# Last stage of a graph network kernel: inverse counts loaded per block, attributes in pieces of nine groups, node layers in another order, 27 packed tiles a run

## Chip, cores and metric

The kernel runs on one core of a Trainium2 chip. Its time is the device time of one execution in microseconds (us), lower is better; the median of three executions is quoted. The engines of the core are TensorE (PE; its weight loads are PEld), VectorE (DVE), ScalarE (ACT), GpSimd (POOL) and SyncE (SP), which issues most of the DMAs.

## Reference

Two layers of message passing over a graph with 6250 nodes of 128 features and 106250 edges sorted by target. The change lies in the second layer, cut here to what it computes:

```python
C = 0.5 * (jnp.cos(edge_weight * (jnp.pi / 5.0)) + 1.0)
C = C * (edge_weight < 5.0)
h = jax.nn.silu(edge_attr @ mlp_w1 + mlp_b1)         # (edges, 64) @ (64, 128)
W = (h @ mlp_w2 + mlp_b2) * C[:, None]
xf = layernorm_relu(x) @ lin1_w
agg_sum = jax.ops.segment_sum(xf[src] * W, dst, num_segments=n_nodes)
cnt = jax.ops.segment_sum(jnp.ones((msg.shape[0],)), dst, num_segments=n_nodes)
agg = agg_sum / jnp.maximum(cnt, 1.0)[:, None]
out = jax.nn.silu(agg @ lin2_w + lin2_b) @ lin_w + lin_b
x = x + out
```

Edges with a weight of 5 or more add nothing. The inputs draw weights from 0 to 20.12, so about a quarter of the edges count ("active" ones).

## Kernel before

The nodes are cut into 49 blocks of 128. Three passes follow one another. Passes 1 and 2 (the first layer, and the rows of the second) go over the edges in slots; beside the slots the kernel counts neighbours into matrix tiles in SBUF (`adjacency`), multiplies them with split tables (L2023), and packs the active edges: the edges lie in 8 runs of 26 groups of 512, and each run's active edges are moved together into `CAP` = 28 tiles of 128, with their attributes turned (64 partitions) in the DRAM tensor `packed_attr`. A test on the chip takes a slow general path where a run has more than 128 times `CAP` active edges; the largest run of these inputs has 3347, as counted from the reference's weights.

The **last stage** (pass 3, code from L2133 on for PE) is a loop over `PG` = 56 packed groups h of four tiles. Its steps for a group:

- POOL issues four indirect gathers of 128 table rows each into one of four ring slots (L975). It waits until `summed` says that the group four before is summed.
- SP loads the group's attributes, 64 partitions by 512 (L773), two groups ahead, into one of three buffers `attr_T`.
- PE multiplies them by `mlp_w1` (`hidden`, L2133, one group ahead), ACT applies silu (L1207), PE makes the filter from a bias product (L2069) and four products (L2073).
- DVE builds a one-hot tile (L1521) and multiplies filter, cut and gathered rows (`packed_message`, four instructions of L1735).
- PE runs six products whose result nothing reads (`unused_products`, L2151, into the bank that the next sum overwrites) and sums the message by target (`sum_packed`, L2140); DVE adds the four windows to the accumulator `acc` (`packed_flush`, L1749).

As soon as the edges of a node block j are all in (`PACKED_UPDATES`, worked out from the shapes) its **node layer** is run beside the groups: DVE scales the identity by the block's inverse counts (L1636), PE spreads them with a product by ones (`scales`, L2056), ACT copies that to SBUF (L1198), DVE multiplies the columns of `acc` by it into `z_T` (L1643), PE multiplies by `lin2` (u, L2062), ACT applies silu (L1201), PE multiplies by `lin` (v, L2065), and DVE adds the bias (L1647) and the block's x (L1651); SP stores the row block (L710) and loads the x of the next (L722). 47 of the 56 groups carry a node layer; two blocks come after the loop. Engines follow their program in order, and semaphores tie them. The order around a group's node layer on DVE is:

```python
packed_onehot(h)
packed_message(h)
if h - 1 in PACKED_UPDATES:
    node_3(PACKED_UPDATES[h - 1], 1)      # bias and x
if h in PACKED_UPDATES:
    diagonal(PACKED_UPDATES[h])
if h:
    packed_flush(h - 1)
if h in PACKED_UPDATES:
    node_3(PACKED_UPDATES[h], 0)          # z_T
```

The filter of group g waits for the message of group g - 2, `v` of block j for the finished row of block j - 1, and the load of x for block j for the row of block j - 3.

## Time and profile before

| | us |
|---|---|
| median of 3 executions | 1630.23 (1620.26 to 1630.88) |
| the profiled execution, device time | 1629.68 |
| its span, first to last instruction | 1627.9 |
| mean granted TensorE clock | 0.905 |
| last stage, first gather to the end | 1271.8 to 1627.9 |

The profiled execution lies 0.6 us below the median. Its span is 1.8 us shorter than its device time, which is what lies around the instructions. Times in rows count from the first instruction. A granted clock of 1 is 2.4 GHz, one of 0.5 is 1.2 GHz, and what lies between is a share of time at either.

### The profile page before, as it was taken

The numbers are of one execution on the slowest core, as the hardware profiler recorded it, in microseconds if no ns is written. First come the engines' busy times: TensorE is split into PE (matmuls) and PEld (weight loads), VectorE is DVE, ScalarE is ACT, GpSimd is POOL, SyncE is SP. The second block draws the span as 40 slices with busy tenths as digits, with TensorE's granted clock in tenths as the row PEclk, the third lists the DMA queues.
The fourth block names the chain that finished last, engine by engine and source line by source line (L and its number), as shares of the span: only waits on it lengthen the run. The fifth ranks groups of instructions, "written<-read, shape, count | busy, mean of one in ns | idle before, by whom it ended". The sixth has DMA issues, their size and how long they took to land.

```text
span 1627.9 us, 35768 instructions
## 1 busy us (share of the span) xinstructions
PE 1374.4 (84%) x11813; PEld 1199.7 (74%) x11813; DVE 813.2 (50%) x2806; ACT 724.9 (45%) x2025; POOL 1123.8 (69%) x1158
## 2 busy tenths in 40 slices
PE   3457999988988899884799999998997899999996
PEld 2246888878888788874799888988986566666664
DVE  3984444545455555443444445434534355555553
ACT  2856665656655666652454345335421221222221
POOL 7577777777777777757667776777675575666661
PEclk9955999999999999985899999999998798998897
DMA  4323455544545655536567657766753232333331
GB/s 115 84 60 87 136 154 172 158 149 141 144 128 157 175 159 155 154 85 184 131 190 207 190 151 199 208 163 173 195 143 83 73 90 77 88 91 84 87 87 34
DMA packets 245643, 217.40 MB, mean 134 GB/s; under 512 B 150236, under 2 KB 201568, under 8 KB 244941
## 3 DMA queue, kind: packets, MB, share of 16 engines
q1 hardware_dynamic: 210125, 142.61, 31.0%
q0 software_dynamic: 35328, 72.42, 16.4%
q8 instruction: 99, 1.62, 0.4%
q14 instruction: 91, 0.75, 0.1%
HBM read 156.61 MB, written 58.31 MB: 132 GB/s over the span
## 4 chain that ended last, share of the span: by engine, by line
PE 57%; DVE 16%; issue 9%; POOL 7%; DMA 4%; ACT 3%; DVEq 1%; SPq 1%; ACTq 1%; POOLq 0%
PE ps_product L2023 21%; PE ps_banks L1971 9%; POOL ring L975 7%; PE ps_banks L1983 5%; PE ps_pack L2000 5%; PE ps_banks L2073 5%; DVE acc L1749 3%; DMA table_in<-node_table 2%; PE ps_banks L2140 2%; PE ps_banks L1988 2%; PE ps_banks L2151 2%; PE ps_node L2062 2%; DVE ring L1735 2%; ACT adjacency L1132 1%; ACT packed_T L1178 1%
## 5 line engine op out<-in xcount | busy, mean ns | idle before, releaser
L975 POOL DMA_INDIRECT ring<-node_table,src_idx x880 | 858.2, 975 | 324.1 <-issue 255.5
L2023 PE MATMUL ps_product<-adjacency,table_parts 128*128 128x232 bf16 x4116 | 508.6, 269 | 0.0
L2023 PEld LDWEIGHTS ps_product<-adjacency,table_parts 128*128 128x128 bf16 x4116 | 403.3, 103 | 12.7 <-DVE table_parts L1557 0.2
L1132 ACT CAST adjacency<-ps_banks 128x550 f32 x448 | 298.5, 666 | 213.9 <-PE ps_banks L1988 190.3
L1971 PE MATMUL ps_banks<-onehot,ring 128*128 128x64 f32 x1760 | 251.9, 291 | 73.0 <-issue 46.6
L975 POOL DMA_INDIRECT ring<-node_table,packed_src x224 | 212.4, 948 | 129.5 <-issue 58.7
L1971 PEld LDWEIGHTS ps_banks<-onehot,ring 128*128 128x128 f32 x1760 | 235.4, 208 | 90.0 <-issue 77.5
L1178 ACT COPY packed_T<-ps_pack 67x64 f32 x832 | 173.4, 208 | 160.5 <-PE ps_pack L2000 54.9
L1546 DVE TENSOR_SCALAR code_onehot<-code_iota,code_T 128x600 bf16<-128x600 bf16 x448 | 169.0, 389 | 130.9 <-PE ps_banks L1988 130.1
L1983 PE MATMUL ps_banks<-code_onehot,lo_onehot 128*128 128x300 bf16 x896 | 200.7, 309 | 20.7 <-ACT adjacency L1132 20.5
L2000 PE MATMUL ps_pack<-pack_onehot,edge_in 128*67 128x64 f32 x1664 | 148.7, 236 | 14.9 <-ACT packed_T L1178 14.5
L2000 PEld LDWEIGHTS ps_pack<-pack_onehot,edge_in 128*67 128x67 f32 x1664 | 130.9, 151 | 17.3 <-issue 16.7
L1735 DVE SCALAR_TENSOR_TENSOR ring<-ps_banks,packed_dst,ring 128x128 f32<-128x128 f32 x224 | 63.2, 345 | 120.3 <-PE ps_banks L2073 114.8
L1983 PEld LDWEIGHTS ps_banks<-code_onehot,lo_onehot 128*128 128x128 bf16 x896 | 97.6, 122 | 27.0 <-DVE code_onehot L1546 14.9
L1988 PEld LDWEIGHTS ps_banks<-code_onehot,lo_onehot 128*128 128x128 bf16 x864 | 101.2, 117 | 21.5
L1988 PE MATMUL ps_banks<-code_onehot,lo_onehot 128*128 128x25 bf16 x864 | 112.6, 221 | 0.0
L1537 DVE TENSOR_TENSOR acc<-acc,ps_banks 128x64 f32 x220 | 47.9, 218 | 100.4 <-PE ps_banks L1971 86.7
L1198 ACT COPY scale_all<-ps_banks 128x128 f32<-128x128 f32 x49 | 13.0, 265 | 189.0 <-PE ps_banks L2056 189.0
L1521 DVE TENSOR_TENSOR pack_onehot<-iota_b,rank 128x256 f32<-128x256 bf16 x208 | 86.0, 418 | 16.4 <-PE ps_pack L2000 16.4
L1521 DVE TENSOR_TENSOR onehot<-iota_b,rel 128x256 f32<-128x256 bf16 x220 | 90.8, 413 | 2.7 <-issue 2.7
L2073 PE MATMUL ps_banks<-mlp_w_sb,hidden_T 128*128 128x128 f32 x448 | 81.6, 338 | 0.0
L2073 PEld LDWEIGHTS ps_banks<-mlp_w_sb,hidden_T 128*128 128x128 f32 x448 | 68.8, 234 | 14.2 <-ACT hidden_T L1207 8.1
(277 smaller groups left out, 1499.0 us busy)
## 6 DMA issues: line engine op xcount, KB each, us to landing
kept_tiles<-adjacency SPq DMA_DIRECT2D x84, 406.0 KB
adjacency<-kept_tiles SPq DMA_DIRECT2D x84, 406.0 KB
edge_in<-in_edge_attr_dram SPq DMA_DIRECT2D x207, 128.0 KB
ring<-node_table,src_idx POOLq DMA_INDIRECT x880
packed_attr<-packed_T SPq DMA_DIRECT2D x8, 896.0 KB
attr_T<-packed_attr SPq DMA_DIRECT2D x56, 128.0 KB, 3.0
node_table<-row_out SPq DMA_DIRECT2D x98, 64.0 KB
ring<-node_table,packed_src POOLq DMA_INDIRECT x224
```

The lines of the kernel that those rows point to most:

```text
L975: gps.indirect_dma_start(to, None, table[c], bass.IndirectOffsetOnAxis(index, 0)).then_inc(gathered[s], 16)
L1132: nc.scalar.copy(adjacency[:, b, :, bass.ds(at, n)].rearrange("p (t b) n -> p t b n", t=2), chunk_banks(m).rearrange("p t (b n) -> p t b n ...
L1178: nc.scalar.copy(packed_T[:, run % 2, bass.ds(at[k], WINDOW)], ps_pack[0:RF, k * WINDOW:(k + 1) * WINDOW]).then_inc(packed_out, 1)
L1521: return vec.tensor_tensor(to, iota[:], of.unsqueeze(2).to_broadcast([P, CHUNKS, WINDOW]), ALU.is_equal)
L1546: vec.tensor_scalar(code_onehot[:, m % CODE_SETS, :], code_iota[:], code_T[:].bitcast(F32)[:, at:at + 1], None, ALU.is_equal).then_inc(chu ...
L1735: last = vec.scalar_tensor_tensor(out=ring[:, s, k, :], in0=ps_filter[:, h % 2, k * P:(k + 1) * P], scalar=packed_cut[:, CHUNKS * h + k:CH ...
L1971: last = mm(ps_window, ring[:, s, k, :], onehot[:, n % 2, k, :], start=(k == 0), stop=(k == CHUNKS - 1))
L1983: last = mm(chunk_banks(m)[:, half, :], left(m), code_onehot[:, m % CODE_SETS, half * HIGH * SPAN:(half + 1) * HIGH * SPAN], start=True, s ...
L1988: last = mm(chunk_banks(m)[:, half, :].rearrange("p (b n) -> p b n", n=SPAN)[:, :, 0], left(m - 1), shared.rearrange("p (b n) -> p b n", n ...
L2000: last = mm(ps_pack[0:RF, k * WINDOW:(k + 1) * WINDOW], edge_in[:, s, k, :], pack_onehot[:, q % 2, k, :], start=True, stop=True)
L2023: product = mm(ps_product[:, 0:COLS], table_parts[:, k, part, :], adjacency[:, buffer_of(c, tile), k, :], start=(k == 0 and part == 0), st ...
L2073: last = mm(ps_filter[:, slot, k * P:(k + 1) * P], hidden_T[:, slot, k, :], mlp_w2_sb[:], start=False, stop=(k == CHUNKS - 1))
```

## The change

- `CAP` goes from 28 to 27, so the last stage has 54 groups and 216 gathers for 56 and 224. 47 of the 54 carry a node layer.
- The inverse counts are turned and stored once, at the end of the start phase, into a DRAM tensor `inv_rows`. In the last stage `load_x(3, j)` loads the block's row of it, spread to 128 partitions, together with its x. `diagonal`, `scales` and the copy on ACT are gone.
- The attributes come in six pieces of nine groups (64 partitions by 4608) into two halves that lie over `adjacency`. The first two are loaded near the end of pass 2, once the last product with `adjacency` is done; the others in the loop, at h = 11, 20, 29 and 38.
- On PE u comes behind the filter and v behind the sum. On DVE `z_T` comes straight behind the flush and the bias and x behind `z_T`.
- After the loop the two left blocks no longer go one after the other; the second has banks of its own for u and v.
- The unused products are kept, six a group, but read `table_parts` in place of `adjacency`, with 256 columns for 232.

```diff
-SUPERS, CAP = 8, 28
+SUPERS, CAP = 8, 27
+PIECE = 9
...
+        attr_pieces = adjacency[0:R].rearrange("r s b n -> r (s b n)").bitcast(F32)[:, 0:2 * PIECE * GROUP].rearrange(
+            "r (s e) -> r s e", s=2)
...
+        def u_bank(j):
+
+            return (ps_pack if j in PACKED_TAIL[1:] else ps_node)[:, 0:P]
+
+        def v_bank(j):
+            return ps_count[:, 0 if j in PACKED_TAIL[1:] else 2, 0:F]
...
                     sp.dma_start(x_in[:, b, :], x_mid[j * P:(j + 1) * P, :]).then_inc(x_block[b], 16)
+                    sp.dma_start(scale_in[:, b, :], inv_rows[j, :].partition_broadcast(P)).then_inc(x_block[b], 16)
...
-            def load_attr_T(h):
-                s = h % 3
-                wait(sp, hidden_done, h - 2)
-                sp.dma_start(attr_T[:, s, :], packed_attr[:, h * GROUP:(h + 1) * GROUP]).then_inc(attr_T_loaded[s], 16)
+            def load_piece(i):
+                if i < PG // PIECE:
+                    wait(sp, hidden_done, PIECE * (i - 1))
+                    sp.dma_start(attr_pieces[:, i % 2, :],
+                                 packed_attr[:, i * PIECE * GROUP:(i + 1) * PIECE * GROUP]
+                                 ).then_inc(piece_loaded[i % 2], 16)
...
-                            for h in range(2):
-                                load_attr_T(h)
+                        if c == 2 and n == SLOT_COUNT[2] - REST_SLOTS + 2:
+                            sp.wait_ge(block_used[2], NB * TILES)
+                            for i in range(2):
+                                load_piece(i)
...
                 for h in range(PG):
-                    if h + 2 < PG:
-                        load_attr_T(h + 2)
+                    if h % PIECE == 2 and h > PIECE:
+                        load_piece(h // PIECE + 1)
...
-            def diagonal(j):
-                wait(dve, scale_done, j)
-                vec.tensor_scalar(scale_diag[:], ident[:], inv_count[:, j:j + 1], None, ALU.mult).then_inc(diag_ready, 1)
...
                 if part == 0:
-                    dve.wait_ge(scale_ready, j + 1)
+                    dve.wait_ge(x_block[b], 16 * in_set(b) + 32 * (j // SETS + 1))
                     wait_acc()
-                    vec.tensor_tensor(z_T[:, b, :], columns(j), scale_all[:], ALU.mult).then_inc(z_ready[3], 1)
+                    vec.tensor_tensor(z_T[:, b, :], columns(j), scale_in[:, b, :], ALU.mult).then_inc(z_ready[3], 1)
...
                     packed_message(h)
-                    if h - 1 in PACKED_UPDATES:
-                        node_3(PACKED_UPDATES[h - 1], 1)
-                    if h in PACKED_UPDATES:
-                        diagonal(PACKED_UPDATES[h])
                     if h:
                         packed_flush(h - 1)
                     if h in PACKED_UPDATES:
                         node_3(PACKED_UPDATES[h], 0)
+                    if h - 1 in PACKED_UPDATES:
+                        node_3(PACKED_UPDATES[h - 1], 1)
...
+            pe.wait_ge(inv_ready, 1)
+            turn(ps_pack[0:NB, 0:P], inv_count[:], ident[:]).then_inc(inv_turned, 1)
...
-                        mm(ps_agg[:, bank, 0:COLS], table_parts[:, 0, 0, :], adjacency[:, 0, 0, :],
+                        mm(ps_agg[:, bank, 0:2 * F], table_parts[:, 0, 0, :], table_parts[:, 0, 1:3, :].rearrange("p t f -> p (t f)"),
                            start=True, stop=True)
...
-                    if h - 1 in PACKED_UPDATES:
-                        node_3(PACKED_UPDATES[h - 1], 0)
                     if h == 0:
                         unused_products(1, WARM_UP)
                         pe.wait_ge(row_ready[2], NB)
                     edge_filter(h, h % 2)
                     if h - 1 in PACKED_UPDATES:
-                        node_3(PACKED_UPDATES[h - 1], 1)
+                        node_3(PACKED_UPDATES[h - 1], 0)
                     if h:
                         wait(pe, flushed[3], CHUNKS * (h - 2))
                         unused_products((h - 1) % 2, KEEP_WARM)
                         sum_packed(h - 1)
-                    if h in PACKED_UPDATES:
-                        scales(PACKED_UPDATES[h])
+                    if h - 1 in PACKED_UPDATES:
+                        node_3(PACKED_UPDATES[h - 1], 1)
```

PE in the loop before, one group with a node layer and the start of the next (lin_sb stands for `lin2` with z_T and for `lin` with z_row):

```order
L2133 MATMUL ps_pack<-attr_T,mlp_w_sb 128x512
L2062 MATMUL ps_node<-z_T,lin_sb 128x128
L2069 MATMUL ps_banks<-b_parts,b_ones 128x512
L2073 MATMUL ps_banks<-mlp_w_sb,hidden_T 128x128 x4
L2065 MATMUL ps_banks<-lin_sb,z_row 128x128
L2151 MATMUL ps_banks<-adjacency,table_parts 128x232 x6
L2140 MATMUL ps_banks<-onehot,ring 128x64 x4
L2056 MATMUL ps_banks<-scale_diag,ones 128x128
L2133 MATMUL ps_product<-attr_T,mlp_w_sb 128x512
```

The same stretch of PE in the changed kernel:

```order
L2149 MATMUL ps_pack<-adjacency,mlp_w_sb 128x512
L2083 MATMUL ps_banks<-b_parts,b_ones 128x512
L2087 MATMUL ps_banks<-mlp_w_sb,hidden_T 128x128 x4
L2075 MATMUL ps_node<-z_T,lin_sb 128x128
L2168 MATMUL ps_banks<-table_parts 128x256 x6
L2157 MATMUL ps_banks<-onehot,ring 128x64 x4
L2079 MATMUL ps_banks<-lin_sb,z_row 128x128
L2149 MATMUL ps_product<-adjacency,mlp_w_sb 128x512
```

The product with z_T moved from ahead of the filter to behind it, the one with z_row behind the sum, and the spreading product is gone.

DVE in the loop before, from one z_T to the first window of the next flush:

```order
L1643 TENSOR_TENSOR z_T<-acc,scale_all 128x128
L1521 TENSOR_TENSOR onehot<-iota_b,packed_dst 128x256
L1735 SCALAR_TENSOR_TENSOR ring<-ps_banks,packed_dst,ring 128x128 x4
L1647 TENSOR_TENSOR row_out<-ps_banks,lin_b_all 128x128
L1651 TENSOR_TENSOR row_out<-row_out,x_in 128x128
L1636 TENSOR_SCALAR scale_diag<-ident,inv_count 128x128
L1742 TENSOR_LOAD packed_base_i
L1749 ISA
L1749 TENSOR_TENSOR acc<-acc,ps_banks 128x64
```

The same stretch of DVE in the changed kernel:

```order
L1663 TENSOR_TENSOR z_T<-acc,scale_in 128x128
L1667 TENSOR_TENSOR row_out<-ps_banks,lin_b_all 128x128
L1669 TENSOR_TENSOR row_out<-row_out,x_in 128x128
L1545 TENSOR_TENSOR onehot<-iota_b,packed_dst 128x256
L1753 SCALAR_TENSOR_TENSOR ring<-ps_banks,packed_dst,ring 128x128 x4
L1760 TENSOR_LOAD packed_base_i
L1767 ISA
L1767 TENSOR_TENSOR acc<-acc,ps_banks 128x64
```

The bias and x left the stretch between message and flush, and the scaled identity is gone.

## Rows read from the trace of the kernel before

**Rows 1.** The page, chain that ended last, shares of the whole span.

```profile
PE 57%; DVE 16%; issue 9%; POOL 7%; DMA 4%; ACT 3%; DVEq 1%; SPq 1%; ACTq 1%; POOLq 0%
```

**Rows 2.** Timeline of one group (start, length, engine, line, idle before it).

```profile
1453.88 0.49 PE L2062 MATMUL ps_node<-z_T,lin_sb 128*128 128x128 f32 x2 [0.29 <-DVE z_T L1643]
...
1455.62 0.39 PE L2065 MATMUL ps_banks<-lin_sb,z_row 128*128 128x128 f32 x2
1455.89 1.13 DVE L1735 SCALAR_TENSOR_TENSOR ring<-ps_banks,packed_dst,ring 128x128 f32<-128x128 f32 x4 [1.72 <-PE ps_banks L2073]
1456.93 0.28 DVE L1647 TENSOR_TENSOR row_out<-ps_banks,lin_b_all 128x128 f32<-128x128 f32 x1
...
1457.46 0.28 DVE L1636 TENSOR_SCALAR scale_diag<-ident,inv_count 128x128 f32<-128x128 f32 x1
...
1457.79 0.49 PE L2056 MATMUL ps_banks<-scale_diag,ones 128*128 128x128 f32 x2 [0.34 <-DVE scale_diag L1636]
1457.82 1.28 DVE L1749 TENSOR_TENSOR acc<-acc,ps_banks 128x64 f32 x4
...
1459.20 0.29 DVE L1643 TENSOR_TENSOR z_T<-acc,scale_all 128x128 f32<-128x128 f32 x1
...
1459.55 0.49 PE L2062 MATMUL ps_node<-z_T,lin_sb 128*128 128x128 f32 x2 [0.22 <-DVE z_T L1643]
```

**Rows 3.** Chain of waits of the last stage (start, length, engine, line).

```profile
1340.17 0.49 PE ps_node L2062 x2
...
1347.27 0.49 PE ps_node L2062 x2
...
1448.12 1.05 PE ps_product L2133 x2
1449.49 1.09 PE ps_banks L2073 x8
1450.58 0.60 PE ps_banks L2151 x6
1451.17 0.86 PE ps_banks L2140 x8
```

**Rows 4.** Stretches: busy us of PE, PEld, DVE, ACT, POOL; granted clock, DMA share, GB/s.

```profile
1300.00:1350.00 50.00, 46.52 (x254) 34.27 (x254) 25.71 (x101) 10.16 (x23) 35.02 (x38) 0.88 0.33 87
```

**Rows 5.** Timeline of the end of pass 2 and the stage's first groups.

```profile
1251.09 0.94 POOL L975 DMA_INDIRECT ring<-node_table,src_idx  x1 [0.30 <-issue]
...
1258.58 1.81 PE L1971 MATMUL ps_banks<-onehot,ring 128*128 128x64 f32 x8
...
1271.76 0.94 POOL L975 DMA_INDIRECT ring<-node_table,packed_src  x1 [19.74 <-DMA node_table<-row_out]
...
1276.79 0.39 PE L2069 MATMUL ps_banks<-b_parts,b_ones 3*128 3x512 bf16 x1
...
1280.49 0.95 POOL L975 DMA_INDIRECT ring<-node_table,packed_src  x1 [0.30 <-issue]
...
1283.04 1.13 DVE L1735 SCALAR_TENSOR_TENSOR ring<-ps_banks,packed_dst,ring 128x128 f32<-128x128 f32 x4 [3.08 <-DMA ring<-node_table,packed_src]
...
1299.30 1.01 POOL L975 DMA_INDIRECT ring<-node_table,packed_src  x1 [0.30 <-issue]
```

**Rows 6.** SP's queue around a store of 64 rows of 14,336 bytes.

```profile
1206.26 0.45 SPq L745 DMA_DIRECT2D packed_attr<-packed_T  x1
...
1207.38 2.09 SPq L710 DMA_DIRECT2D node_table<-row_out  x1
```

**Rows 7.** The stretch in which that store moved, columns as in Rows 4.

```profile
1207.40:1212.40 5.00, 5.00 (x56) 4.63 (x54) 0.67 (x6) 0.00 (x0) 3.58 (x4) 0.93 0.92 184
```

**Rows 8.** DMAs of the attributes, issue to landing, us min/median/max.

```profile
DMA to landing us min/median/max: 2.6/3.0/3.8
```

**Rows 9.** Timeline of the end.

```profile
1611.86 1.81 PE L2140 MATMUL ps_banks<-onehot,ring 128*128 128x64 f32 x8
...
1623.65 0.29 DVE L1651 TENSOR_TENSOR row_out<-row_out,x_in 128x128 f32<-128x128 f32 x1
```

More of the change, by code:

```diff
@@ L533, in gnn_kernel @@
         held = sem("held")
-        attr_T_loaded = [sem(f"attr_T_loaded_{s}") for s in range(3)]
+        piece_loaded = [sem(f"piece_loaded_{b}") for b in range(2)]
         edge_turned = sem("edge_turned")
@@ L696, in _, with store_inverse @@
             store_table(0)
+            def store_inverse(time):
+                sp.wait_ge(early_done, time + 1)
+                if time:
+                    sp.wait_ge(inv_stored, 16)
+                sp.dma_start(inv_rows, inv_out).then_inc(inv_stored, 16)
             def late_params():
@@ L841, in fast_path @@
                 first = NB - len(PACKED_TAIL)
-                store_row(3, first - 1)
-                for j in PACKED_TAIL:
-                    if j + 1 < NB:
-                        load_x(3, j + 1)
+                for j in PACKED_TAIL[1:]:
+                    load_x(3, j)
+                for j in range(first - 1, NB):
                     store_row(3, j)
@@ L1287, in general_path @@
                 start_sums(1)
+                act.wait_ge(inv_stored, 16)
+                act.wait_ge(inv_turned, 2)
+                nc.scalar.copy(inv_out, ps_pack[0:NB, 0:P]).then_inc(W12_ready, 1)
                 act.wait_ge(early_done, 2)
@@ L2051, in node_2 @@
                     mm(bank[:, 2 * P:2 * P + F], h2_T[:, b, :], lin1_sb[:], start=True, stop=True).then_inc(xf_done, 1)
-            def scales(j):
-                pe.wait_ge(diag_ready, j + 1)
-                wait(pe, row_ready[3], j)
-                mm(ps_count[:, 2, P:2 * P], ones[:], scale_diag[:], start=True, stop=True).then_inc(scale_done, 1)
             def node_3(j, part):
@@ L2061, in node_3 @@
                     pe.wait_ge(z_ready[3], j + 1)
-                    mm(ps_node[:, 0:P], lin2_sb[:], z_T[:, b, :], start=True, stop=True).then_inc(u_done, 1)
+                    wait(pe, u_ready, j)
+                    mm(u_bank(j), lin2_sb[:], z_T[:, b, :], start=True, stop=True).then_inc(u_done, 1)
                 if part == 1:
                     pe.wait_ge(u_ready, j + 1)
-                    mm(ps_count[:, 2, 0:F], z_row[:, b, :], lin_sb[:], start=True, stop=True).then_inc(v_done, 1)
+                    wait(pe, row_ready[3], j - 1 if j in PACKED_TAIL[1:] else j)
+                    mm(v_bank(j), z_row[:, b, :], lin_sb[:], start=True, stop=True).then_inc(v_done, 1)
             def edge_filter(g, slot):
@@ L2130, in hidden @@
                 def hidden(h):
-                    pe.wait_ge(attr_T_loaded[h % 3], 16 * (h // 3 + 1))
+                    piece, at = divmod(h, PIECE)
+                    if at == 0:
+                        pe.wait_ge(piece_loaded[piece % 2], 16 * (piece // 2 + 1))
                     wait(pe, hidden_ready, h - 1)
-                    mm(hidden_bank(h), mlp_w1_sb[:], attr_T[:, h % 3, :], start=True, stop=True).then_inc(hidden_done, 1)
+                    mm(hidden_bank(h), mlp_w1_sb[:], attr_pieces[:, piece % 2, at * GROUP:(at + 1) * GROUP],
+                       start=True, stop=True).then_inc(hidden_done, 1)
                 def sum_packed(h):
```

77 lines of the change are left out of this document (37 added, 40 removed).

## Prediction

> **What bounds the kernel now.** I read the chain that ended last first: 57% of it is PE, 16% DVE, 7% POOL [rows 1]. That is a mean over three passes, and the change touches almost only the last stage, 1271.8 to 1627.9. So I took the timeline of one of its groups and followed who waits for whom [rows 2]. PE starts u (L2062) at 1453.88 and again at 1459.55: a group with a node layer takes 5.67 us. What closes the circle is one chain over two engines: u, filter, message on DVE (1455.89), bias and x, scaled identity (1457.46), flush (1457.82, 1.28 us), z_T (1459.20), and again u, which waits for it. Neither engine alone is full. PE's own work in a group is, by the steps of the chain of waits [rows 3], 1.05 for `hidden`, 0.32 for the bias product (from 1449.17 to 1449.49), 1.09 for the filter, 0.60 for the unused products and 0.86 for the sum, 3.92 us; u adds 0.49, v 0.39 and the spreading product 0.49 [rows 2]. That is 5.29 of 5.67 us.
>
> Second, TensorE's clock. From 1300 to 1350 it was granted at 0.88 [rows 4], so about a quarter of that time ran at 1.2 GHz. A group in which it falls takes 7.10 us (1340.17 to 1347.27, [rows 3]) for 5.67: a fall costs 1.43 us. The loop runs from 1276.79 [rows 5] to the last sum at 1611.86 [rows 9], 335.1 us. 47 groups with a node layer at 5.67 (266.5) and 9 without at 3.92 (35.3) leave 33.3 us, some 23 falls.
>
> Third, POOL. The 1st and the 23rd gather of the stage start at 1271.76 and 1299.30 [rows 5]: while POOL waits for nothing, a gather takes 27.54 / 22 = 1.252 us and a group 5.01 us. Before, POOL had 0.66 us of slack in a group; it is the next bound behind the chain.
>
> **The change, part by part.**
>
> *Reordering.* z_T is still made behind the flush, but u now stands behind the filter, so the filter and with it the next message no longer wait for z_T. What is left of the old circle lacks u (0.43 from start to start), the scaled identity and the two row additions (1456.93 to 1457.82, 0.89): 5.67 - 0.43 - 0.89 = 4.35 us, under what PE itself needs. PE then needs 3.92 + 0.49 + 0.39 = 4.80, and the unused products with 256 columns for 232 add 10% of 0.60, 0.06: 4.86 us with a node layer, 3.98 without. DVE's work (message 1.13, flush 1.28, z_T 0.29, row additions 0.57, one-hot some 0.4) is under 4 us and its waits fit in: the flush waits for the sum, z_T and rows follow, and the next filter ends about 3 us after that sum. New on PE's way: v waits for the previous block's row, which DVE ends 2 to 3 us after the sum before, so about 2 us early; u waits for z_T with about 1 us to spare. Nothing queued behind them waits as long as these hold.
>
> *Sum for PE.* 47 x 4.86 + 7 x 3.98 = 256.3 us, from 1276.79: the last sum would end at 1533.1 at full clock and with no wait.
>
> *Sum for POOL.* 216 gathers. The last starts at 1271.76 + 215 x 1.252 = 1540.9. A message starts 2.55 us after its group's last gather (1280.49 to 1283.04, [rows 5]), so at 1543.5. Then message 1.13, flush 1.28, z_T 0.29, u 0.49 and the last sum 0.86: 1547.6. So POOL, not PE, is the nearer bound: 5.01 against 4.86 us in a group. PE has 14.5 us to lose in the whole loop before it counts.
>
> *Clock.* What will the falls be? Between none and the 0.41 a group of before (22 of them, 31.5 us). Before, PE stood still in every group for z_T; now it is busy 4.86 of 5.01 us, and only the 7 groups without a node layer leave 1 us. I take 10 falls, 14.3 us: those 7 places and a few after the holds below. The Trainium skill ("TensorE: Matmul & The Clock Gate", section "HAM oscillation") says that a kernel whose matmul bursts are parted by idle gaps falls back to the half clock, and a dense stream keeps the full one; the direction is that of my 10 against 22.
>
> *Attribute pieces.* As many bytes, but 64 rows of 18,432 bytes at a time. The nearest row is a store of 64 rows of 14,336: after it SP needed 2.09 us to issue its next DMA [rows 6], and for 5.0 us the DMA engines were 92% busy at 184 GB/s [rows 7]. A piece is 1.29 times as large: 6.4 us in which a gather may land late. The lower end is nothing, as the 128 KB loads (3.0 us from issue to landing, [rows 8]) and the gathers now share without a wait. I take the store's row, the only one with such long packets. The first hold then stops PE for up to 6.4 us. The three later ones meet a PE that already runs behind its gathers (it makes up 0.15 us in a group and 1 us in one without a node layer, some 2 us between two pieces), so I count one hold, 6.4 us. SP stands too, 2 to 4 us, and the loads of x and inverse behind the piece come later: they are issued almost two groups, 9.4 us, before z_T needs them, and take 1.0 us to issue and 3.0 to land, so 5.4 us are free.
>
> *Together.* 1533.1 + 14.3 + 6.4 = 1553.8 for the end of the last sum, later than POOL's 1547.6, so this one counts.
>
> *End.* Before, from the end of the last addition (1623.94, [rows 9]) to the span's end there were 4.0 us, the store. After the last sum come now flush and two z_T, of which the last waits for x of block 48: its load waits for row 45, about 0.8 us before the sum's end (1546.8 for 1547.6), and lands 4.0 us later; then z_T 0.3, u and v 0.8 each at the low clock, silu 0.4, additions 0.6, waits 0.4 and the store 4.0. That ends 10.4 us after the sum, for 14.2 before.
>
> *Pieces 0 and 1 in pass 2.* They go out at about 1241, together 12.8 us of transfer. PE summed the pass's last slot at 1258.58, its last gather was issued at 1251.09 [rows 5]; less 2.55 that is 5 us of cover. Between no delay and 7.9 us I take 1.5, since most held gathers land well ahead of that sum. *Start phase.* One transpose, one copy of 49 rows and a small store: a few tenths of a us beside work that the chain has anyway; nothing. One transpose less in each `turn_packed`, beside 27: nothing. The second load per block is 0.5 us on SP, which the attribute load of before took as well.
>
> Sum: 1553.8 + 10.4 + 1.5 = 1565.7 of span, and 1.8 around it: **1567 us** for the profiled 1629.68, which stands for the median (1630.23).
>
> **The rivals.**
>
> *Clock as before.* Nothing shows what density keeps the clock; the falls could stay at 0.41 a group. Then 31.5 for 14.3 us: 1585.
>
> *Every piece is paid in full.* If PE never runs behind, or a hold lasts longer than the row says, the loop pays 4 x 6.4 for 6.4 (+19.2) and pass 2 its 7.9 for 1.5: 1593. For it speaks the 92% of [rows 7]. A rule of the Trainium skill says more: "DMA: Bandwidth & Descriptors", section "Queues, rings and completion order", lets an engine change queues only between packets of several descriptors, so that a gather waits for the whole share of the piece that lies ahead of it. By that rule the hold is the transfer's 6.4 us each time, and the time 1593 unless the lag hides it; by the 128 KB loads alone it would be 1561. With the clock as before as well it would be 1610.
>
> *The load of x and inverse becomes the bound (slower).* z_T of block j + 1 needs two DMAs that are issued when row j - 2 is done. Two groups less 0.6 us must hold 1.0 us of issue and the landing: at 3.0 to 3.8 us [rows 8] this asks for 2.7 us a group and decides nothing. The kernel gets slower from 6.3 us a group on, which means a landing of 11 us for each of 49 blocks; at 12 us it would be about 1656. Against it: nothing in the stage lands so late.
>
> *It doesn't do what it says.* A run of over 3456 active edges would take the general path. The largest has 3347, so no.
>
> **How the numbers follow.** Forecast 50% (1558 to 1575, its lower end being POOL's bound 1547.6 + 10.4 + 1.8 = 1560 less what executions differ), clock as before 20%, pieces in full 20%, both 5%, the load as bound or another wait in the circle that leaves it within 1% 2.5%, slower 2.5%. The range of 8 in 10 is 1555 to 1598: it leaves out both together and the last two. A measurement of this kernel can tell about 1% (16 us) from no change; faster by more 0.95, within it 0.025, slower 0.025.
>
> **What would show it.** Groups about 5.0 us apart, with DVE's L1753 or PE's sum waiting for the gathers (DMA ring) now and then, and POOL issuing with no wait for sums; the last gather near 1541; a granted clock of 0.93 or more in the loop for 0.88; gathers that land late after each `adjacency<-packed_attr` near h = 11, 20, 29, 38; PE never idle for z_T. It would be wrong if POOL still waited for sums most of the time (PE is the bound: more falls, or a wait that I haven't seen), or if the stage began after 1276.

## Result, and the profile after

The changed kernel takes 1562.02 us (median of 4 runs, 1557.33 to 1565.6), the kernel before beside it 1630.56 (4 runs, 1620.26 to 1642.73). The ratio is 0.959 (95% interval 0.954 to 0.964), 68.5 us less. The forecast was 1567 with a range of 1555 to 1598. The profiled execution took 1565.6 us, its span 1563.9.

The chain that ended last, on the page of after, by engine and by line:

```profile
PE 52%; POOL 16%; DVE 10%; issue 10%; DMA 5%; ACT 4%; SPq 1%; ACTq 1%; DVEq 1%; POOLq 0%
```

Against [rows 1] PE and DVE fall (57% and 16% before) and POOL goes from 7% to 16%: the gathers (now L1002) have taken over a part of the path. The same chain in the loop alone, from 1280 to 1545, by line (the profile cuts the line off at its end); first before, then after:

```profile
by line: PE ps_banks L2073 22.7%; DVE acc L1749 12.6%; PE ps_banks L2140 8.5%; PE ps_banks L2151 8.2%; issue 8.1%; DVE ring L1735 7.1%; PE ps_node L2062 7.0%; PE ps_banks L2069 5.6%; DVE z_T L1643 4.2%; PE ps_banks L2065 2.9%; DVEq L1749 2.
```

```profile
by line: POOL ring L1002 62.3%; issue 20.3%; DMA ring<-node_table,packed_src 3.5%; PE ps_banks L2157 2.6%; PE ps_banks L2168 2.4%; PE ps_banks L2087 2.3%; PE ps_pack L2149 1.5%; PE ps_node L2075 1.1%; DVE ring L1753 0.8%; PE ps_product L214
```

Before, the chain runs through PE and DVE and no gather stands in the line. After, the gathers and their issue are over 80% of it. From the first sum to the last a group took 6.01 us before (1281.15 to 1611.86, 55 steps) and takes 5.12 us after (1281.58 to 1552.75, 53 steps).

A group late in the stage. Timeline of after: start, length, engine, line, operation, and in brackets the idle time before it with what ended it.

```profile
1500.05 0.44 PE L2079 MATMUL ps_banks<-lin_sb,z_row 128*128 128x128 f32 x2
...
1500.42 1.12 PE L2149 MATMUL ps_product<-adjacency,mlp_w_sb 64*128 64x512 f32 x2
...
1501.47 0.39 PE L2083 MATMUL ps_banks<-b_parts,b_ones 3*128 3x512 bf16 x1
...
1501.73 0.29 DVE L1663 TENSOR_TENSOR z_T<-acc,scale_in 128x128 f32<-128x128 f32 x1
...
1501.79 1.16 PE L2087 MATMUL ps_banks<-mlp_w_sb,hidden_T 128*128 128x128 f32 x8
...
1502.78 0.39 PE L2075 MATMUL ps_node<-z_T,lin_sb 128*128 128x128 f32 x2
...
1503.01 0.82 PE L2168 MATMUL ps_banks<-table_parts 128*128 128x256 bf16 x6
...
1503.66 1.00 PE L2157 MATMUL ps_banks<-onehot,ring 128*128 128x64 f32 x8
...
1504.50 0.44 PE L2079 MATMUL ps_banks<-lin_sb,z_row 128*128 128x128 f32 x2
```

Read the PE rows from one v (L2079) to the next: 1500.05 to 1504.50, 4.45 us, and no PE matmul shows an idle time in front of it. z_T is ready at 1502.02 and u (L2075) starts at 1502.78, so nobody waits for z_T here; in [rows 2] that wait closed the circle. In the whole loop (1277 to 1554.2) PE still waits for z_T ten times, 18.9 us together, most of it where a gather comes late. The start-to-start steps say what each product costs in a full stream: v 0.37, `hidden` 1.05, bias 0.32, filter 0.99, u 0.23, unused products 0.65, sum 0.84.

What happens when a piece of attributes goes out, in the timeline of after (SPq is SP's DMA issue):

```profile
1331.93 0.45 SPq L794 DMA_DIRECT2D adjacency<-packed_attr  x1
...
1335.67 0.95 POOL L1002 DMA_INDIRECT ring<-node_table,packed_src  x1 [0.30 <-issue]
...
1342.04 1.12 DVE L1753 SCALAR_TENSOR_TENSOR ring<-ps_banks,packed_dst,ring 128x128 f32<-128x128 f32 x4 [5.19 <-DMA ring<-node_table,packed_src]
...
1344.46 0.29 DVE L1663 TENSOR_TENSOR z_T<-acc,scale_in 128x128 f32<-128x128 f32 x1
...
1344.81 0.69 PE L2075 MATMUL ps_node<-z_T,lin_sb 128*128 128x128 f32 x2 [4.04 <-DVE z_T L1663]
1345.29 1.49 PE L2168 MATMUL ps_banks<-table_parts 128*128 128x256 bf16 x6
```

The message's last gather is issued at 1335.67 and the message starts 6.37 us later, for 2.55 us in [rows 5]: the gather came 3.8 us late. PE stood 4.04 us for z_T, and after that the clock is down: six unused products take 1.49 us for 0.82. The six pieces, over the whole kernel:

```profile
L794 SPq DMA_DIRECT2D adjacency<-packed_attr x6: 450/462/874, 1238.3 to 1471.0; - x6
...
DMA to landing us min/median/max: 8.5/8.9/15.0
```

Issuing one costs SP 0.46 us; it lands after 8.9 us (15.0 where two were issued together, in pass 2). Over the 9 us in which the piece of 1331.93 is on its way the DMA engines are 92% busy (columns as in [rows 4]):

```profile
1331.90:1340.90 9.00, 8.59 (x53) 5.91 (x51) 3.08 (x12) 1.78 (x4) 6.84 (x8) 1.00 0.92 194
```

The two pieces in pass 2 had an effect as well. There the changed kernel was 2.3 us ahead of the kernel before (a sum at 1248.36 for 1250.63). Then the next sum waited for its gathers, which were issued just behind the two pieces:

```profile
1254.32 1.94 PE L1988 MATMUL ps_banks<-onehot,ring 128*128 128x64 f32 x8 [3.94 <-DMA ring<-node_table,src_idx]
```

The pass's last sum came at 1258.71 for 1258.58 [rows 5], so the lead was gone. The waits of after from 1280 to 1545 (who waited for what: us in total, times, longest):

```profile
POOL ring L1002 <- issue: 62.5, 205, 0.3
...
DVE ring L1753 <- DMA ring<-node_table,packed_src: 34.3, 19, 5.2
DVE acc L1767 <- PE ps_banks L2157: 29.7, 38, 2.2
PEld ps_node L2075 <- DVE z_T L1663: 16.5, 9, 4.2
DVE ring L1753 <- PE ps_banks L2087: 16.2, 23, 2.5
```

POOL waits 205 times for no more than its own 0.3 us of issue, so it hardly ever waits for a sum; the messages wait for the gathers 19 times, 34.3 us. And the stretches of the loop, to be read beside [rows 4] (busy us and instructions of PE, weight loads, DVE, ACT, POOL; then granted clock, DMA share, GB/s):

```profile
1300.00:1350.00 50.00, 45.28 (x275) 32.62 (x273) 28.24 (x112) 9.40 (x19) 37.79 (x41) 0.96 0.46 109
1350.00:1400.00 50.00, 46.26 (x272) 33.76 (x272) 29.17 (x114) 10.04 (x19) 37.80 (x41) 0.89 0.47 112
1400.00:1450.00 50.00, 49.27 (x292) 35.91 (x290) 30.47 (x118) 10.19 (x19) 35.53 (x38) 0.90 0.44 105
1450.00:1500.00 50.00, 45.99 (x266) 33.44 (x266) 27.51 (x107) 9.14 (x17) 37.85 (x40) 0.86 0.46 111
1500.00:1550.00 50.00, 48.19 (x317) 35.71 (x316) 32.82 (x127) 10.56 (x20) 35.70 (x37) 1.00 0.40 92
```

The end of the loop, which answers to [rows 9]:

```profile
1545.79 0.95 POOL L1002 DMA_INDIRECT ring<-node_table,packed_src  x1 [0.31 <-issue]
...
1549.66 1.13 DVE L1753 SCALAR_TENSOR_TENSOR ring<-ps_banks,packed_dst,ring 128x128 f32<-128x128 f32 x4 [2.67 <-DMA ring<-node_table,packed_src]
1550.70 1.27 DVE L1767 TENSOR_TENSOR acc<-acc,ps_banks 128x64 f32 x4
...
1552.75 1.43 PE L2157 MATMUL ps_banks<-onehot,ring 128*128 128x64 f32 x8
...
1556.77 0.29 DVE L1663 TENSOR_TENSOR z_T<-acc,scale_in 128x128 f32<-128x128 f32 x1 [0.78 <-DMA scale_in<-inv_rows]
```

The last message waits for the last gathers. The stage's first gather starts at 1271.38, 0.4 us earlier than before (1271.76). The last sum starts at 1552.75 for 1611.86 (59.1 us less), and from there to the end of the span it is 11.1 us for 16.0 (4.9 less). That is the whole difference of the two spans, 64.0 us. Of the 59.1 us, two groups fewer at 6.01 us are some 12, and shorter groups (5.12 for 6.01 us) are some 47.

### The profile page after: what moved, and what is told of

Same layout as the page of the kernel before. It is cut to its first block, busy times and chain, and to the rows that moved or that the text cites. A ratio compares the mean times of both kernels' runs of the same rounds, so it can differ in the third digit from the quotient of the medians.

```text
span 1563.9 us, 35264 instructions
## 1 busy us (share of the span) xinstructions
PE 1322.5 (85%) x11658; PEld 1161.2 (74%) x11658; DVE 797.0 (51%) x2739; ACT 712.0 (46%) x1975; POOL 1119.4 (72%) x1150
## 4 chain that ended last, share of the span: by engine, by line
PE 52%; POOL 16%; DVE 10%; issue 10%; DMA 5%; ACT 4%; SPq 1%; ACTq 1%; DVEq 1%; POOLq 0%
PE ps_product L2040 23%; POOL ring L1002 16%; PE ps_banks L1988 9%; PE ps_banks L2000 6%; PE ps_pack L2017 5%; DMA table_in<-node_table 2%; PE ps_banks L2005 2%; ACT packed_T L1207 1%; ACT adjacency L1161 1%; DMA src_raw<-in_src_dram 1%; PE ps_node L2068 1%; DVE z_row L1642 1%; DVE z_row L1655 1%; PE ps_pack L2025 1%; PE ps_node L2065 1%
## 5 line engine op out<-in xcount | busy, mean ns | idle before, releaser
L1002 POOL DMA_INDIRECT ring<-node_table,src_idx x880 | 859.6, 977 | 319.4 <-issue 255.2
L1002 POOL DMA_INDIRECT ring<-node_table,packed_src x216 | 206.6, 956 | 90.8 <-issue 64.7
L2005 PEld LDWEIGHTS ps_banks<-code_onehot,lo_onehot 128*128 128x128 bf16 x864 | 101.2, 117 | 21.5
L1561 DVE TENSOR_TENSOR acc<-acc,ps_banks 128x64 f32 x220 | 47.7, 217 | 98.4 <-PE ps_banks L1988 83.8
L1767 DVE TENSOR_TENSOR acc<-acc,ps_banks 128x64 f32 x216 | 47.8, 221 | 53.2 <-PE ps_banks L2157 31.1
L1642 DVE SCALAR_TENSOR_TENSOR z_row<-ps_node,dinv,b_all 128x128 f32<-128x128 f32 x48 | 16.8, 349 | 105.0 <-PE ps_node L2062 102.5
L2087 PE MATMUL ps_banks<-mlp_w_sb,hidden_T 128*128 128x128 f32 x432 | 66.2, 299 | 0.0
```

The source lines that it names most:

```text
L1002: gps.indirect_dma_start(to, None, table[c], bass.IndirectOffsetOnAxis(index, 0)).then_inc(gathered[s], 16)
L2005: last = mm(chunk_banks(m)[:, half, :].rearrange("p (b n) -> p b n", n=SPAN)[:, :, 0], left(m - 1), shared.rearrange("p (b n) -> p b n", n ...
L2087: last = mm(ps_filter[:, slot, k * P:(k + 1) * P], hidden_T[:, slot, k, :], mlp_w2_sb[:], start=False, stop=(k == CHUNKS - 1))
```

## Experiments

e1 to e4 ran on one chip, which I call B, e5 to e8 on another (C), e9 to e12 on a third (D). I call A the chip of the times above; the record has no number for it, so it may be a fourth one, or one of the three in another condition. On B, C and D the kernel before takes 1996.88, 1993.65 and 2023.46 us (7 runs each) for 1630 on A, 22 to 24% more, and the changed kernel on C takes 25% more than on A. So all comparisons are ratios to the kernel before on the same chip, or between kernels of one chip, and the experiments say what the parts are worth there. On A only the whole change was timed. The expectations were written in numbers of A, or guess at one of these chips; below, their differences are compared.

**e1: 28 tiles (chip B).** The capacity goes back to 28 tiles a run, so there are 56 packed groups for 54; pieces of eight, since nine doesn't divide 56.

```diff
-    SUPERS, CAP = 8, 27
-    PIECE = 9
+    SUPERS, CAP = 8, 28
+    PIECE = 8
```

> The changed kernel with 28 tiles a run again (56 groups, 224 gathers, seven pieces of eight groups, all else kept). Theory: with the circle over z_T cut, POOL's gathers set the pace (5.01 us a group), so two groups more cost 8 gathers, 10 us: about 1572. Rival (TensorE sets the pace, at the 4.45 us of the trace after): 9 us, hardly to be told apart here; this run only prices the 27 tiles. If the 27 tiles were the main part of the 64 us gained, it would be above 1590.

Measured: 1954.49 us (4 runs, 1947.97 to 1956.16), ratio 0.978 (0.972 to 0.983).

**e2: pieces of three groups (chip B).** Packets of 6,144 bytes for 18,432, and 18 loads for 6.

```diff
-    PIECE = 9
+    PIECE = 3
...
-                    if h % PIECE == 2 and h > PIECE:
+                    if h % PIECE == 0 and h:
```

> The changed kernel with the attributes in 18 pieces of three groups (393 KB each) for six of nine. Theory: each hold of the gathers shrinks to about a third and hides in the two gathers' lead, the 8 to 9.5 us gaps between sums at the pieces go away, but since TensorE makes up 0.56 us a group after each hold, only the last group's delay and some clock falls are gained: about 1558, between 1553 and 1562. Rival (each hold is paid in full, some 4 to 5 us for each of four): 1542 to 1546.

Measured: 1950.43 us (4 runs, 1947.65 to 1957.66), ratio 0.978 (0.973 to 0.984).

**e3 and e7: the old order (chips B and C).** u goes back in front of the filter and v behind the filter; on DVE the row additions go back in front of the flush. All else stays as changed.

```diff
+                    if h - 1 in PACKED_UPDATES:
+                        node_3(PACKED_UPDATES[h - 1], 0)
                     edge_filter(h, h % 2)
                     if h - 1 in PACKED_UPDATES:
-                        node_3(PACKED_UPDATES[h - 1], 0)
+                        node_3(PACKED_UPDATES[h - 1], 1)
                     if h:
                         wait(pe, flushed[3], CHUNKS * (h - 2))
                         unused_products((h - 1) % 2, KEEP_WARM)
                         sum_packed(h - 1)
-                    if h - 1 in PACKED_UPDATES:
-                        node_3(PACKED_UPDATES[h - 1], 1)
```

> The changed kernel with the order of before on TensorE (u ahead of the filter, v ahead of the unused products) and on VectorE (bias and x ahead of the flush), all else kept. Theory (the order cut the circle u, filter, message, flush, z_T): a group takes 5.67 less the 0.28 of the scaled identity, 5.4 us, and the clock falls of before return: 1590 to 1605. Rival (the gain came from dropping the spreading product, the copy on ScalarE and the scaled identity, or from the loads): under 1572.

Measured on B: 1970.77 us (4 runs, 1966.2 to 1979.96), ratio 0.988 (0.982 to 0.994).

> The changed kernel with the order of before on TensorE and VectorE, again, now beside the changed kernel on one chip. Theory: a group at 5.4 us and the clock falls of before, 28 to 42 us over the changed kernel. Rival (the order is worth little): under 10 us over it.

Measured on C: 1974.46 us (4 runs, 1964.63 to 1984.09), ratio 0.989 (0.983 to 0.994).

**e4 and e8: three gathers (chips B and C).** Three of the four gathers of a packed group are issued, and the waits for them count three; the fourth part of `ring` keeps old rows, so these runs are only for the time.

```diff
-                    for k in range(CHUNKS):
+                    for k in range(3):
```

> The changed kernel with three gathers a group for four in the last stage; the fourth part of each message multiplies rows left over in the ring, so 27000 of the 108000 products of the layer use wrong rows and the output isn't the reference's. Theory (POOL is the bound, TensorE needs 4.45 us a group): groups go to 4.45 us and the holds are met from a full ring: last sum near 1520 to 1525, time 1532 to 1540. Rival (TensorE and its clock are the bound, POOL only close behind): above 1555.

Measured on B: 1863.06 us (2 runs, 1859.67 to 1866.46), ratio 0.933 (0.927 to 0.940).

> The changed kernel with three gathers a group for four in the last stage, again; a quarter of the rows of the messages are left over from before. Theory (POOL is the bound): 22 to 30 us under the changed kernel on this chip, sums 4.45 us apart. Rival (TensorE and its clock are): under 7 us.

Measured on C: 1868.88 us (2 runs, 1864.65 to 1873.11), ratio 0.936 (0.931 to 0.941).

**e5: the changed kernel itself (chip C).**

> The changed kernel itself, beside the kernel before on the chip of this call, so that the other runs of the call are read against it. In the call before this one both engines' hand-overs took longer on that chip and the kernel before took 1997 us. If this chip is like the first: 1562 and 1630. If it is like the second: the changed kernel near 1950 for 1997.

Measured: 1953.0 us (4 runs, 1946.5 to 1955.45), ratio 0.977 (0.973 to 0.981). The same change that gives 4.1% on A gives 2.3% here.

**e6: the old spreading in the new order (chip C).** The inverse rows in DRAM and their loads are gone; scaled identity, product with ones and ACT's copy are back, in front of each z_T.

```diff
-                    sp.dma_start(scale_in[:, b, :], inv_rows[j, :].partition_broadcast(P)).then_inc(x_block[b], 16)
...
+                    if h in PACKED_UPDATES:
+                        diagonal(PACKED_UPDATES[h])
                     if h:
                         packed_flush(h - 1)
...
+                    if h in PACKED_UPDATES:
+                        scales(PACKED_UPDATES[h])
```

> The changed kernel with the inverse counts spread as before (scaled identity on VectorE ahead of the flush, a product by ones on TensorE behind v, a copy on ScalarE) and no inverse rows in DRAM; order, pieces and 27 tiles kept. Theory (the order cut the circle; TensorE has 0.56 us of room in a group under POOL's 5.01): TensorE goes to 4.45 + 0.4 us, still under POOL, so 0 to 8 us over the changed kernel on the same chip. Rival (dropping these three steps gave the gain): 25 us or more over it.

Measured: 1955.47 us (4 runs, 1934.28 to 1960.12), ratio 0.977 (0.970 to 0.984).

**e9: the order alone (chip D).** The kernel before, with nothing but the new order of u, v, row additions, flush and z_T. (The spreading product then waits for ACT's copy of the block before it, and v for the row before it, as the order needs.)

```diff
-                    if h - 1 in PACKED_UPDATES:
-                        node_3(PACKED_UPDATES[h - 1], 0)
...
                     edge_filter(h, h % 2)
                     if h - 1 in PACKED_UPDATES:
-                        node_3(PACKED_UPDATES[h - 1], 1)
+                        node_3(PACKED_UPDATES[h - 1], 0)
...
                         sum_packed(h - 1)
+                    if h - 1 in PACKED_UPDATES:
+                        node_3(PACKED_UPDATES[h - 1], 1)
```

> The kernel before with nothing changed but the order of the node layer in the last stage: u behind the filter, v behind the sum, the row additions behind the flush and z_T. The inverse is still spread by a scaled identity and a product, the attributes come group by group, 28 tiles, 232 columns in the unused products. If the order is the whole of the gain, it stands where the changed kernel does: ratio to before 0.958 to 0.962 on a chip like that of the first runs, 0.977 on one like those of e1 to e8. If the four parts add up (the order undone alone cost 1.1% of the 2.3% on these chips), it gains about 1.1%: ratio 0.989. If the order only works together with the spreading taken off PE, it gains nothing: 1.00.

Measured: 1994.24 us (4 runs, 1987.63 to 2002.1), ratio 0.989 (0.984 to 0.995).

**e10: two gathers (chip D).** As e4, with `range(2)`.

> The changed kernel with two of the four gathers of each packed group left out (half of the rows that enter the sums are then stale). Three gathers took 84 to 90 us off on these chips. If the gathers set the pace by their number at any count, the second takes as much again: about 1780 us where before is 1995. If with three PE was already the bound (its work in a group is 4.45 us, the period with three was 4.90), only what is left of the late hand-overs can go: 0 to 25 us, 1845 to 1870 us. On a chip like that of the first runs: from 1562 down to some 1530 to 1540, no lower, as PE's 4.45 us a group hold.

Measured: 1859.51 us (2 runs, 1858.09 to 1860.93), ratio 0.921 (0.915 to 0.927).

**e11 and e12: none and ten unused products (chip D).**

```diff
-KEEP_WARM = 6
+KEEP_WARM = 0
```

> The changed kernel without the six unused products in each group of the last stage (0.66 us of PE at the full clock). If the unused products earn their keep through the clock, the granted clock of the last stage falls by 0.1 or more and the kernel gets slower by 10 to 40 us (0.5 to 2%). If PE's own length counts in a group and the clock holds, it gets faster by up to 54 x 0.6 = 32 us. If the gathers are the bound and the clock holds, nothing moves: within 5 us of the changed kernel.

Measured: 1985.55 us (4 runs, 1974.86 to 1986.36), ratio 0.982 (0.976 to 0.987).

```diff
-KEEP_WARM = 6
+KEEP_WARM = 10
```

> The changed kernel with ten unused products in each group for six: 0.44 us more of PE, 4.9 us in a group at the full clock, under the 5.01 us of the gathers. If the falls of the clock can be bought off by denser work, the clock of the last stage rises and the time falls by 5 to 15 us. If PE's length counts directly, it gets slower by 54 x 0.44 = 24 us. If neither counts, within 5 us of the changed kernel.

Measured: 1959.58 us (4 runs, 1957.89 to 1964.32), ratio 0.971 (0.966 to 0.976).

## What the experiments show

**The order is worth about half on these chips, and it adds up.** Put back alone it costs 1.1% (0.989 on C for the changed kernel's 0.977 there: 21.5 us; on B it stands 16 to 20 us behind e1 and e2). Put in alone it gains 1.1% (e9, 0.989). So the other parts together bring the remaining 1.2% or so, whether the order is there or not; each of these ratios is known to 0.4 to 0.7%. The theory had asked for 28 us or more from the order (e3, e7); the 21.5 us on C are less, and more than its rival's 10.

Whole times also contain passes 1 and 2, and there the traces of one chip scatter: the last stage's first gather comes between 1574 and 1584 on B and between 1578 and 1589 on C. So I set the last stage beside them, read from the one trace of each run (us; the last column is from the start of the last sum to the end of the span):

| run, chip | first gather | first gather to the end | last sum to the end |
|---|---|---|---|
| before, A | 1271.8 | 356.1 | 16.0 |
| after, A | 1271.4 | 292.5 | 11.1 |
| e1, 28 tiles, B | 1574.2 | 380.1 | 12.0 |
| e2, pieces of 3, B | 1579.5 | 366.3 | 11.5 |
| e3, old order, B | 1579.2 | 389.9 | 11.4 |
| e5, changed, C | 1579.0 | 374.7 | 10.7 |
| e6, old spreading, C | 1578.2 | 375.9 | 13.4 |
| e7, old order, C | 1582.5 | 392.4 | 11.2 |
| e9, order alone, D | 1596.0 | 389.9 | 15.7 |
| e11, none unused, D | 1600.5 | 383.7 | 10.7 |
| e12, ten unused, D | 1606.6 | 351.7 | 10.6 |

By the stage alone the old order costs 17.7 us on C.

**Which of the others it is, isn't shown, but two can be priced.** By whole times 28 tiles for 27 (e1, 0.978) and the old spreading for the loaded rows (e6, 0.977) each cost nothing that can be told from the changed kernel's 0.977. Those intervals are 10 to 14 us wide to each side, and the price forecast for e1 was 10 us, so e1's ratio doesn't speak against it. The stages do speak: e1's is 13.8 us longer than that of e2 on the same chip (which differs by its pieces as well), and two groups of some 6.5 us are 13 us. The end of the loop takes 15.7 us in e9, which has the old one, and 10.5 to 12.0 in all other runs on these chips but e6 (13.4), so the new end with its loaded rows is worth 4 to 5 us. Together that is an estimate of some 18 us of the 24 us that 1.2% are. e6's stage is 1.2 us longer than e5's: the spreading costs little in the loop, as its expectation of 0 to 8 us had it. Pieces of three (e2, 0.978) weren't timed beside pieces of nine on one chip, and 8 us between the two stages is a difference across chips, so what the long packets cost there stays open. What no run undid alone are the attribute loads group by group (54 loads for 6), the new end, and the width of the unused products (256 columns for 232).

**PE's own work, with its six unused products, is a floor of 4.4 us a group.** With two gathers the stage's gathers run from 1600.4 to 1835.3, 107 intervals or 4.39 us a group. Its timeline shows v after v:

```profile
1705.16 0.44 PE L2079 MATMUL ps_banks<-lin_sb,z_row 128*128 128x128 f32 x2
...
1705.59 0.95 POOL L1002 DMA_INDIRECT ring<-node_table,packed_src  x1 [3.34 <-PE ps_banks L2157]
1706.84 0.95 POOL L1002 DMA_INDIRECT ring<-node_table,packed_src  x1 [0.30 <-issue]
...
1709.61 0.44 PE L2079 MATMUL ps_banks<-lin_sb,z_row 128*128 128x128 f32 x2
...
1710.05 0.95 POOL L1002 DMA_INDIRECT ring<-node_table,packed_src  x1 [2.26 <-PE ps_banks L2157]
```

4.45 us, as on A; here POOL waits for PE's sums (50 times from 1610 to 1835, 116.1 us), and PE for z_T only four times, 4.9 us. The 4.39 us are the mean expected of 47 groups at 4.45 and 7 without u and v at 3.96 (on A two steps around such a group take 4.23 and 4.18 us in place of twice 4.45). The second gather taken away therefore brought little (0.921 for 0.936, some 30 us, across two chips), where the first brought 84 us on C.

**The 84 us are no confirmation of the gathers' bound on A.** The theory had asked for 22 to 30 us there, with groups at 4.45 us; groups with three gathers take 4.84 us (C) and 4.68 us (B). And with four gathers the gathers don't set the pace on C: a group takes 6.52 us (1579.0 to 1929.4, 215 intervals) for the 5.0 us that POOL alone needs, and POOL waits for others 38 times from 1600 to 1930, 90.8 us:

```profile
POOL ring L1002 <- PE ps_banks L2157: 62.0, 23, 4.3
```

and the 28.8 us below. What bounds the loop on A is thus read from A's trace alone: 205 of 208 gathers wait for nothing, and the chain runs through them.

**On B, C and D engines wait without a releaser that the profile shows.** Some groups of the changed kernel on C, in the timeline:

```profile
1702.57 0.39 PE L2075 MATMUL ps_node<-z_T,lin_sb 128*128 128x128 f32 x2
...
1703.44 1.00 PE L2157 MATMUL ps_banks<-onehot,ring 128*128 128x64 f32 x8
...
1707.46 0.37 ACT L1226 ACTIVATE z_row<-ps_node,lin_b_col 128x128 f32<-128x128 f32 x1 [3.58 <-remote]
1707.49 1.12 DVE L1753 SCALAR_TENSOR_TENSOR ring<-ps_banks,packed_dst,ring 128x128 f32<-128x128 f32 x4 [4.49 <-remote]
1707.84 0.95 POOL L1002 DMA_INDIRECT ring<-node_table,packed_src  x1 [2.05 <-remote]
1707.88 0.49 PE L2079 MATMUL ps_banks<-lin_sb,z_row 128*128 128x128 f32 x2 [3.44 <-ACT z_row L1226]
```

u ends at 1702.96 and the sum at 1704.44, but ACT, which needs only u and is free from 1703.89 on, starts at 1707.46, and DVE and POOL within 0.4 us of it. PE then stands 3.44 us for ACT. The profile names no releaser ("remote"). On A the same steps wait for PE's results, and neither trace of A has one such row; that PE's results come late here is how I read it, and the profile doesn't show it. The waits of this kind on C from 1600 to 1930:

```profile
ACT hidden_T L1232 <- remote: 51.6, 8, 13.5
...
DVE ring L1753 <- remote: 45.8, 11, 4.6
ACT z_row L1226 <- remote: 43.6, 11, 6.3
...
POOL ring L1002 <- remote: 28.8, 15, 3.1
```

With DVE's flush (19.0) that is 189 us summed over the engines, which wait at the same time. With three gathers 12.4 us are left (e8, 1600 to 1850), with two it is one wait of 2.8 us. So in this stage such waits nearly vanish when fewer rows are gathered. More can't be said. It isn't gathers issued without a pause that bring them: on C POOL pauses (above), and in passes 1 and 2 of e8, where nothing was taken away, POOL has 101 such waits, 136.2 us. Nor do they set the length of a group by themselves. With the old order on C (e7) only 45.7 us of them are left from 1600 to 1930, and a group takes 6.67 us; with ten unused products (e12) they sum to 169.5 us in 315 us, and a group takes 6.05. What causes them, and why A has none, the records don't tell.

**The clock and the unused products.** The stretch from 1610 to 1925, same columns as above; first the changed kernel (six, chip C), then none, then ten (both chip D):

```profile
1610.00:1925.00 315.00, 267.45 (x1346) 189.52 (x1345) 142.56 (x549) 47.83 (x89) 180.09 (x190) 0.80 0.34 82
```

```profile
1610.00:1925.00 315.00, 276.72 (x1025) 191.96 (x1023) 137.85 (x528) 46.15 (x86) 178.66 (x190) 0.62 0.33 79
```

```profile
1610.00:1925.00 315.00, 269.83 (x1640) 195.43 (x1638) 147.37 (x573) 49.77 (x92) 196.99 (x210) 0.94 0.35 86
```

Granted clock 0.62, 0.80 and 0.94 for none, six and ten; the groups take 6.62, 6.52 and 6.05 us. Ten beat none by 26 us on one chip (1959.58 for 1985.55; 32 us by the stages), although they are 1.1 us more of PE in a group. Against six the gain is 0.6% by the ratios (0.971 for 0.977), across two chips and with intervals that overlap, and six against none is 0.5%, also across chips, where 0.5 to 2% was expected. e12 has the lowest ratio of the whole kernels tried there, but it didn't run on A, where the clock of the loop is 0.91 already.

## Why the prediction was right, and where it wasn't

**POOL as the nearer bound: right.** Groups came 5.10 us apart for 5.01. The last gather started at 1545.8, forecast 1540.9: of the 4.9 us POOL spent 4.1 in three waits for PE's sum. The last message (1549.66) waited 2.67 us for its gathers. The forecast had let PE's line, with its falls and its hold, end last (1553.8) and POOL's at 1547.6; it was POOL's, late, that ended the loop, with the last sum's end at 1554.2 for 1553.8. The two lines end close together, though: from 1498 to 1542 the sums follow each other at PE's own 4.2 to 4.45 us, and PE meets the gathers again only in the last two groups. No run on A takes gathers away, so by how much POOL is the nearer bound there isn't shown.

**PE's need of 4.86 us in a group: wrong, it is 4.45.** The step "PE then needs 3.92 + 0.49 + 0.39" took whole durations of u and v, 0.88, where a matmul in a full stream costs what lies between its start and the next one's: 0.23 and 0.37, 0.60 together. In front of u the filter also takes 0.99 for the 1.09 us of a group without it, so the two add some 0.5 us, not 0.88. A group without them is 3.96 us by the steps of 4.23 and 4.18 above, for 3.98 forecast; that part was right. So PE makes up 0.56 us in a group behind POOL, not 0.15.

**"I count one hold": wrong in count and in size, 11.5 us of PE for 6.4, and it hardly mattered.** The neighbouring sums after three of the four pieces stand 8 to 9.5 us apart instead of 5, and PE stood 4.04, 3.62 and 3.84 us there. Behind the piece of 1430.41 it stood only 0.73 us, since it was running behind its gathers, which is how the forecast had let three of the four go by. The transfer was mis-sized too: the 6.4 us gave the piece all of the 184 GB/s of [rows 7], while in the 9 us behind the issue at 1331.93 some 1.75 MB moved at 194 GB/s (the row 1331.90:1340.90), of which the piece is 1.18 MB, the rest gathers and other loads. A held gather came 3.8 us late. With 0.56 us gained per group PE was nearly back at the gathers before the next piece. The rival *every piece is paid in full* was nearer in count (three of four) and wrong in the bill: 1593 for 1566. The rule that I set beside it (the Trainium skill, "DMA: Bandwidth & Descriptors", section "Queues, rings and completion order") agrees in direction with the gather that came 3.8 us late behind the piece of 1331.93. Engines that are 92% busy would hold a gather up as well, and no run tells the two apart.

**"I take 10 falls, 14.3 us": the count was near, the price wrong.** From 1280 to 1545 the granted clock is 0.91, so some 48 us of 265 ran at 1.2 GHz (twice the missing 0.09), which is some 24 us of work for the 14.3 forecast; before it is 0.89 of 330 us from 1280 to 1610, some 73. By the length of their unused products 8 of the 53 groups run at the low level, in four stretches, against some 20 groups in a dozen stretches before. Each stretch began behind a stand-still of PE, 1.55 us at 1290.55 and the three above. One of the four:

```profile
1390.00:1409.00 19.00, 18.71 (x67) 13.27 (x68) 8.40 (x32) 2.48 (x5) 13.17 (x14) 0.50 0.35 83
```

There PE is 98% busy and a group takes 8.38 us for 4.45 (unused products at 1390.88, 1399.26 and 1407.64), so a group at the low level costs 3.9 us. The forecast's 1.43 us was read from groups that spent a part of their 5.67 us waiting. The forecast of "0.93 or more" was not reached. Again the slack paid: at the gathers' pace PE can be slow without anybody waiting, until a message is late.

**The end and pass 2: near.** After the last sum's end 9.7 us for 10.4, with z_T waiting 0.78 us for its load, as described. The two pieces in pass 2 took 2.4 us where I had put 1.5: a lead of 2.3 us over the kernel before had turned into a lag of 0.1 by the pass's last sum. As that lead wasn't in the forecast, the stage still began 0.4 us earlier than before.

**That PE's line was met to 0.4 us is luck.** PE was cheaper (0.41 us in each of 47 groups, 19 us) and lost more to the clock (24 us for 14.3) and to waits (18.9 us for 6.4), so the errors nearly cancelled: 1554.2 for 1553.8. POOL's line was forecast to within 4.9 us, and that isn't luck. The slower rival (loads of x and inverse) never showed: the one wait for `scale_in` inside the loop is under 2 us. The sum itself, 1567 for 1562 to 1566, was good in part by this luck, and in part because the nearer bound, which alone gives 1560, had been read from gathers that wait for nothing.

**What it missed.** That the same change brings 2.3% where before takes 1994 us, and that there the gathers don't set the pace. Nothing in the profile of before points to it.

## What to carry to other kernels

When a circle through two engines is cut, work out the next bound from an engine that already runs without a wait; its start-to-start time is exact, while a sum of durations on PE is too large by the overlap of each product with the next (here 0.28 of 0.88 us for two small products). Slack on one engine is what pays for its stalls: on A three holds and 48 us of half clock left the loop's end within 7 us of the 1547.6 forecast from the gathers alone, because PE had half a us to spare in each group. The price of a fall of the clock depends on that slack too: 1.43 us a group where PE was waiting anyway, 3.9 us where it wasn't. And a gain read on one chip is that chip's: time a change on another before you rank its parts.

## What was not expected of the hardware

- Before takes 1630 us in one place and 1994 to 2023 on three chips, with the same 0.95 us for a gather's issue and the same 4.45 us for PE's full group. The slower ones show waits for which the profile names no releaser (189 us summed over the engines from 1600 to 1930 in e5, none on A), several at once, up to 4.5 us in the rows above. In the last stage they nearly vanish with three or two gathers for four; how much of the 22 to 24% they are, no run shows.
- 1152 KB in rows of 18,432 bytes take 8.9 us from issue to landing, and a gather behind them comes 3.8 us late (A).
- Ten products whose results nobody reads make the kernel faster than none, by 26 us, with the granted clock at 0.94 for 0.62 (D). Elsewhere (A) the clock fell to its lower level behind stand-stills of 1.55 to 4.04 us, and in one stretch it stayed there for 19 us in which PE was 98% busy.
